# A message-passing block in fp32 on one core: another opening, plain points in the third group, the second period unrolled

## The reference

```
# layer 0, per graph, x: 256 x 128, A: 256 x 256
h      = relu(bn1(conv1d(x^T, conv1_w)))                # 1 tap
x_conv = relu(bn2(conv1d(h, conv2_w, pad=8)) + x^T)^T   # 17 taps, 128 -> 128 channels
s      = x @ w_se.T + b_se                              # 3 columns
A      = exp(-|s_n - s_m|^2) * adj
x_nmp  = A @ relu(x @ w_msg.T + b_msg)
gi     = [x_conv, x_nmp] @ w_ih.T + b_ih ; gh = x @ w_hh.T + b_hh
r, z   = sigmoid(gi_r + gh_r), sigmoid(gi_z + gh_z)
n      = tanh(gi_n + r * gh_n)
x      = layernorm(x + (1 - z) * n + z * x)
# layer 1
h      = relu(((1 + eps) * x + adj @ x) @ W1 + b1)
x      = layernorm(x + h @ W2 + b2)
```

## Time and profile before

| | |
|---|---|
| median of 3 runs | 387.81 us (386.9 to 388.11) |
| profiled execution | 386.43 us, its span 384.5 us |
| PE busy | 363.2 us (94%), 2150 matmuls |
| DVE busy | 326.4 us (85%), 669 instructions |
| ACT busy | 232.1 us (60%) |
| POOL busy | 222.5 us (58%) |
| DMA | 19.39 MB, mean 50 GB/s |

### The profile page before, as it was taken

How to read it: one execution, slowest core, us unless ns; L and a number is a source line. 1 busy time by engine, 2 the same in 40 slices (tenths; PEclk the granted TensorE clock), 3 DMA queues, 4 the chain that set the end, 5 groups by cost and what they waited for, 6 DMA issues and landing times.

```text
span 384.5 us, 6418 instructions
## 1 busy us (share of the span) xinstructions
PE 363.2 (94%) x2150; PEld 315.1 (82%) x2150; DVE 326.4 (85%) x669; ACT 232.1 (60%) x435; POOL 222.5 (58%) x195
## 2 busy tenths in 40 slices
PE   3969997999999999999999999999999999999994
PEld 1847876798888998989888898989888998988973
DVE  4999999999699986999689986999879996994584
ACT  4454445664866566673776558574676648555765
POOL 3246273698328763597437963396536983286352
PEclk9996999999999999999999999999999999999999
DMA  7500004030110210120101301130101201000002
GB/s 245 213 0 3 0 0 141 26 112 1 56 55 18 94 40 17 55 111 0 55 5 49 109 0 55 55 108 3 55 1 56 109 3 55 3 0 2 0 29 82
DMA packets 7991, 19.39 MB, mean 50 GB/s; under 512 B 672, under 2 KB 5024, under 8 KB 6944
## 3 DMA queue, kind: packets, MB, share of 16 engines
q1 hardware_dynamic: 7536, 18.50, 13.6%
q10 hardware_dynamic: 432, 0.59, 0.5%
HBM read 14.90 MB, written 4.19 MB: 50 GB/s over the span
## 4 chain that ended last, share of the span: by engine, by line
PE 61%; DVE 30%; issue 5%; DMA 1%; ACT 1%; POOL 1%; SPq 0%; DVEq 0%; ACTq 0%
PE back L1266 26%; PE conv L1266 17%; PE back L1379 6%; DVE stats L1015 3%; PE back L1474 3%; DVE stl L844 3%; DVE tail L1050 2%; PE front L1351 2%; DVE wl L1077 2%; DVE adjT L1120 2%; PE back L1430 2%; DVE sv L865 1%; DVE nmpl L844 1%; DMA tail<-in_conv_dram 1%; PE front L1371 1%
## 5 line engine op out<-in xcount | busy, mean ns | idle before, releaser
L1266 PE MATMUL conv<-sth,wh 128*128 128x256 f32 x217 | 65.4, 301 | 1.9 <-DVE stl L844 1.8
L1266 PE MATMUL conv<-stl,wh 128*128 128x256 f32 x217 | 61.8, 285 | 0.0
L1266 PE MATMUL conv<-sth,wl 128*128 128x256 f32 x217 | 61.7, 284 | 0.0
L538 POOL TENSOR_TENSOR rstd<-rstd,minus_half 128x4 f32<-128x4 f32 (+1 forms) x34 | 38.3, 1127 | 35.3 <-DVE rstd L1019 34.7
L559 POOL TENSOR_TENSOR amat<-amat,adjT 128x512 f32<-128x512 f32 x32 | 50.6, 1609 | 5.4 <-ACT amat L682 5.4
L543 POOL TENSOR_TENSOR xw<-xw,xv 128x512 f32<-128x512 f32 (+1 forms) x17 | 21.4, 1256 | 48.4 <-ACT xw L706 48.4
L1266 PEld LDWEIGHTS conv<-sth,wh 128*128 128x128 f32 x217 | 40.9, 189 | 4.6 <-DVE stl L844 1.7
L1266 PEld LDWEIGHTS conv<-stl,wh 128*128 128x128 f32 x217 | 41.1, 189 | 0.1
L1266 PEld LDWEIGHTS conv<-sth,wl 128*128 128x128 f32 x217 | 40.8, 188 | 0.0
L638 ACT ACTIVATE sth<-sv 128x272 fp32r<-128x272 f32 (+1 forms) x33 | 17.3, 523 | 33.6 <-DVE sv L865 21.5
L567 POOL TENSOR_TENSOR adjT<-adjT,diag 128x256 f32<-128x256 f32 x32 | 28.0, 903 | 8.0 <-DVE diag L1166 8.0
(11 more groups left out here) (232 smaller groups left out, 1033.0 us busy)
## 6 DMA issues: line engine op xcount, KB each, us to landing
adjT<-in_adj_dram SPq DMA_DIRECT2D x8, 1024.0 KB, 4.8
out_dram<-tail SPq DMA_DIRECT2D x15, 256.0 KB, 2.1
xv<-in_x_dram SPq DMA_DIRECT2D x7, 512.0 KB, 3.3
gbuf<-in_gates_dram SPq DMA_DIRECT2D x1, 576.0 KB, 7.4
tail<-in_conv_dram ACTq DMA_DIRECT2D x2, 256.0 KB, 4.0
xv<-in_x_dram SPq DMA_DIRECT2D x2, 256.0 KB, 4.8
later_w<-in_later_dram SPq DMA_DIRECT2D x1, 452.0 KB, 6.2
tail<-in_conv_dram SPq DMA_DIRECT2D x1, 320.0 KB, 5.2
```

What stands on the lines that cost most here:

```text
L538: done(pool.tensor_tensor(rstd[:, k, v, q], rstd[:, k, v, q], minus_half[:, q], ALU.pow), RSTD[k])
L1266: ins = pe.matmul(bank, a, b, start=first and k == 0, stop=last and k == len(todo) - 1)
```

## The change

Ten things, all in the opening and the first two periods:

1. Loads: the conv weights' first piece is issued before the second half of x; the third piece goes to ACT's queue; `later_w` is cut in two, the message part (264 columns) on ACT's queue, the second layer's part (semaphore `mlp_loaded`) on SP's behind x of group 1, where the identity also goes. SP no longer waits for the conv weights before it loads group 1's x.
2. `first_diffs(g)` makes both token differences on DVE, for groups 0 and 1; POOL makes none in the opening.
3. Group 0's PLUS1 and MINUS1 streams are made on DVE (`first_stream1`), between the tap sums.
4. On DVE `factors(0)` stands ahead of `parts1(0)`, the second x low part of group 0 behind `u_sum(0)`.
5. On PE the transposes of the factors stand ahead of MINUS2, and the four distances stand together behind it; ACT's exps follow them, with the tap copies behind.
6. `diag` is made by ACT from the identity; eps1 = 1 + eps in place in the vectors.
7. The combined taps of HALF and PLUS2 lie in `first_w` (which grows by nine blocks; PLUS2's lie over conv1's weights) and not in the gates' buffer. Their high parts are the last of ACT's opening, their low parts are made at the end of the second period's `pair1_add` (`second`), and group 2's HALF and PLUS2 points are plain.
8. In the first period `stream_low(1, 2)`, before in the opening, follows `parts1`; DVE's `gates` is cut into `reset` and `add_input`, with the low parts of taps between; `u_sum(1)` moves behind `h_low(0)`, `pair2_add(1)` behind the x splits.
9. On POOL the diagonal adds of group 0 wait in two pairs (for ACT's first `nmp_high` and for DVE's first message sum of group 1), and `x_low1` of group 1 moves into the first period, one half behind each of the two `rsqrt`.
10. The loop covers periods 3, 4 and 5, 6; the second period, steady(2), stands ahead of it.

The core of the diff:

```diff
             steady(1, 1, True)
+            steady(2, 0, True)
             with eng.Fori(0, (GROUPS - 4) // 2) as i:
-                steady(i * 2 + 2, 0, True)
                 steady(i * 2 + 3, 1, True)
-            steady(GROUPS - 2, 0, True)
+                steady(i * 2 + 4, 0, True)
...
-        W_ORDER = ("conv1", "gates", HALF, PLUS2, PLUS1, ZERO, MINUS2, MINUS1, INF, "w1")
+        W_ORDER = ("conv1", "gates", PLUS1, MINUS2, ZERO, MINUS1, INF, "w1", HALF, PLUS2)
...
 # SP prologue
                 sp.dma_start(xv[0][:, cols(0)], x_v[0, :, cols(0)]).then_inc(x_pair0_loaded, 16)
+                sp.dma_start(c2raw[:, 0:5, :], t["conv2"][:, 0:5, :]).then_inc(conv2_loaded, 16)
                 done(sp.dma_start(xv[0][:, cols(1)], x_v[0, :, cols(1)]), X_LOADED)
-                sp.dma_start(c2raw[:, 0:5, :], t["conv2"][:, 0:5, :]).then_inc(conv2_loaded, 16)
-                sp.dma_start(c2raw[:, 5:9, :], t["conv2"][:, 5:9, :]).then_inc(conv2_loaded, 16)
-                sp.dma_start(later_w[:, :], t["later"]).then_inc(later_loaded, 16)
-                sp.wait_ge(conv2_loaded, 64)
                 wait(sp, X_LOADED, 0, 16)
                 load_x(1, 1)
+                sp.dma_start(ident, t["consts"]).then_inc(consts_loaded, 16)
+                sp.dma_start(later_w[:, W1_AT:], t["later"][:, W1_AT:]).then_inc(mlp_loaded, 16)
...
 # DVE, steady
+                reset(gb, 0)
+                if first:
                     tap_low(MINUS2)
-                gates(gb, 1 - u, 0)
-                if first:
-                    tap_low(MINUS1)
+                add_input(gb, 0)
                 gates_end(gb, 0)
...
+                if second:
+                    tap_low(HALF)
+                    tap_low(PLUS2)
...
 # PE, steady
-                if not first:
+                if second:
+                    plain_taps(gm, HALF)
+                    taps(gm, ZERO)
+                    plain_taps(gm, PLUS2)
+                elif not first:
```

223 lines of the change are left out of this document (131 added, 92 removed).

## The result

The changed kernel takes 383.39 us, the median of four runs (383.15 to 383.65); the kernel before took 387.36 us in four runs (386.59 to 388.11). The ratio is 0.9898, 95% interval 0.9874 to 0.9921, so the gain is 4.0 us with an interval from 3.1 to 4.9. The forecast was 383.0, a gain of 4.8 against the median of 387.81 shown ahead. Timed again later the changed kernel took 383.24 us against 386.77 (ratio 0.9916, 0.99 to 0.9931), a gain of 3.5 us. Over the experiments 33 further runs of the kernel before have medians of 386.58 to 386.77, so the 387.36 above lies high, and the gain is nearer to 3.5 us than to 4.0.

A forecast was written before the change was run, and what follows sets the result against it. VectorE's instruction list was taken to bound until 93.67 us, TensorE afterwards. Opening -4.1, first period -1.5, plain points +0.3, second period +0.7, boundary wait -0.2 gave -4.8: 383.0 us from 387.81, range 379.9 to 386.2.

The forecast's parts named there:

- Loads: Opening: the new load order costs nothing, -0.3 to +0.5 us; x's second half is hidden if landed by about 7.7.
- DVE's first differences: Opening: DVE making both of group 0's token differences alone takes 1.3 us where one half took 1.89; -0.6 us.
- Taken off and put on DVE's list: Opening: weight splits, diag and a stream split leave DVE, -2.5 us; group 1's differences, two streams, x's low part come, +2.8.
- Masks: Opening: POOL's masks start near 25.6 us instead of 28.39 and hit DVE less; -0.7 us, from -1.6 to +0.5.
- Contention that goes: Opening: with POOL idle from 16 to 25 us, factor steps save 1.9 us and two tap sums 1.2; -3.1 us.
- First period with the plain points: First period -1.5 us from factor steps without POOL neighbours and earlier gates; group 2's unsplit HALF and PLUS2 points +0.3.
- Second period: HALF and PLUS2 low splits, now ahead of the first output sum, cost +0.7 us, from 0 to +2.6.
- Unrolling: Period loop: changing which bodies stand inside it costs 0 us, as the number of bodies in the code stays the same.
- Collisions come back: Rival, opening and first period: POOL's masks, streams and adds meet DVE's moved two-input instructions; 385.7 us, chance 0.20.
- DVE stops binding: Rival, opening and first period: POOL's work misses DVE almost wholly, only PE's work is left; 380.5 us, chance 0.13.
- Paid back: Rival: second period's splits cost 2.6 us and late PE gates lose half the opening's gain; 387.0 us, chance 0.07.
- The clock's case: Rival, opening before group 1's gates: PE pauses, its clock falls to half rate; slower, 389.5 us, chance 0.05.

The follow-up runs named there:

- experiment 10: Changed kernel with x's second half loaded before conv weights, both periods' low splits moved earlier, POOL's masks held until the last tap sum: 381.37 us, ratio 0.9869.
- Experiment 1: Changed kernel with the second half of group 0's x issued ahead of the first conv weights again: 383.53 us, ratio 0.992.
- Experiment 7: Changed kernel plus two POOL tensor operations on unread scratch beside DVE's group 0 factor steps: 385.74 us, ratio 0.9971.
- experiment 8: Changed kernel with half of group 0's and both of group 1's token differences back on POOL: 385.08 us, ratio 0.9962.
- Experiments 3: Changed kernel with POOL's two splits of group 1's x back behind the opening's diagonal adds: 383.81 us, ratio 0.9931.
- 6: Changed kernel with the low halves of INF's and W1's weights split earlier in the first period, before group 0's residual addition: 382.39 us, ratio 0.9889.
- Experiment 2: Changed kernel with the second period's HALF and PLUS2 low splits between reset product and first gates' add: 382.59 us, ratio 0.9893.
- experiment 11: Changed kernel with HALF and PLUS2 weights split in the opening, group 2's points split again, and the period loop as before: 383.61 us, ratio 0.9923.

## Why the prediction was right, and where its terms were off

The forecast of 383.0 us and its direction held, and so did the main mechanism: GpSimd's work beside VectorE's factor steps and tap sums went, and both early stretches became shorter. The gain is 4.0 us against 4.8; the terms were off by more than that, on both sides.

Part of the agreement is luck. Between the two profiled executions, for which the sum was made, the forecast was -4.8 and the result is -2.9, and 0.7 of that is a shortening of the later periods that the sum had at nothing. The medians show 4.0 because the kernel before ran high in those four runs; against its later medians the gain is 3.2 to 3.5 us.

**Loads: nothing forecast, +0.7 measured.** The bound I gave was +0.5, and "h1 later than 10.9 us" was named as a sign of error; DVE's first difference, for which it waits, starts at 11.53. The step that failed is "hidden if it lands by about 7.7 us": x's second half landed at 8.3. It cost PE more than the wait, too. PE's HALF point of group 0 starts 2.0 us later than before (15.78 for 13.78): conv1 ends 0.9 later (10.43 for 9.57), and the products between it and the point take 1.1 more. Here are the message products of the kernel before, of the changed kernel and of experiment 10 (count, busy us, mean ns):

```profile
L1351 PE MATMUL front<-later_w,xv 128*128 128x132 f32 x12 | 2.4, 372 | 0.0
```

```profile
L1400 PE MATMUL front<-later_w,xv 128*128 128x132 f32 x12 | 2.8, 427 | 0.0
```

```profile
L1407 PE MATMUL front<-later_w,xv 128*128 128x132 f32 x12 | 1.5, 276 | 0.0
```

The delay is still there when the PLUS2 point of group 0 starts (21.43 us for 19.56), which the distances and exps follow, and so the masks start at 27.5 and not at the 25.6 us that I gave. Experiment 1 gave that earlier start, and showed that it is worth 0.2 us at the end of the opening.

By the Trainium skill (DMA: Bandwidth & Descriptors, Issuing engines are not separate DMA queues) loads of several engines share the same 16 DMA engines and interleave. The trace fits that, with a landing anywhere from just ahead of 8.03 to 9.30 us in nine executions of one order; that the interleaving makes the landing loose is not shown by any run.

**DVE's first differences, -0.6: right.** Two in 1.36 us (11.53 to 12.89) where I gave 1.3.

**Taken off and put on DVE's list, -2.5 and +2.8: about right, but collisions were left out.** DVE's busy time in the opening fell by 4.1 us (39.34 to 35.26; its stretch begins in both at the first tap work, 8.33 and 8.36). Group 1's differences took 0.92 and 1.78 us beside the masks, 2.6 in place of 1.3, and x's second low part 1.24 in place of 0.7. These are hits by the masks, which the sum has in the next term.

**Masks, -0.7 forecast, -0.2 measured.** The term was mis-sized, and it doesn't follow from its own parts: one hit less is -0.9, the diagonal adds +0.6, together -0.3. In the trace three old hits went (the last tap sum 1.77 to 0.82, the first wv 1.50 to 0.43, the usum sum ahead of it 1.76 to 1.25, together -2.5), and new ones came: x's low part and the differences as above (+1.9), the last usum pair beside POOL's streams and diagonal adds 2.30 for 1.87 (+0.4).

**Contention that goes, -3.1: right.** Factor steps 2.91 to 0.97 (-1.9), two tap sums 2.85 to 1.67 (-1.2). Experiment 7 brings the neighbours back and the time with them. By experiment 8 the reason isn't the move of group 1's differences to DVE: in the new order its h1 is there only at 28.4 us, when the factor steps are long done, and the PLUS1 and MINUS1 streams need parts1, which now stands behind the factors. The order alone keeps both away from the factor steps.

**The sum of the opening, -4.1 forecast, -2.8 measured:** +0.7 from the loads, +0.5 from the masks term. TensorE's gates at 45.35 us stayed under the 45.5 that I gave as the limit.

**First period with the plain points, -1.2 forecast, -0.8 measured; the parts were wrong more than the sum.** The factor steps gave -2.6 (3.86 to 1.28) for -2.9, and the 2.0 us gate wait went. The collision that I feared for the pair sums, +1.3, didn't come: the masks of this period end at 76.73, and the pair takes 1.29 us at 79.42. Before, it took 3.46 us beside the masks and the x splits ahead of it 2.88, for 1.28 now, so here 3.8 us went that the forecast hadn't counted. The collision came 10 us earlier. POOL's x split, put between the norm steps, pushed POOL's additions and masks into DVE's low splits, and the three rows at 68.55 to 71.60 us cost some 3 us over what they take alone (4.70 in all). The INF stream's first step at 58.91 us meets POOL's gate product too, 1.51 us for 0.43. In all DVE's busy time fell by 2.0 us (43.88 to 41.90), and only 0.8 of that came: PE's waits fell from 3.7 to 2.9 us, and they set the period, not the sum of DVE's list, by which I had reckoned. I priced the moved split at its old place only; its new one I called free, "the x split between the norm steps". Experiments 3 and 6 show both ends: back at its old place it costs 0.4 more, and with the low weights out of its way 0.9 less.

By the Trainium skill (GPSIMD Engine Reference, Specifications) it is DVE instructions with two SBUF inputs, or in a two-port mode, that contend with POOL. The trace agrees: those three have two SBUF inputs, and the four usum rows at 73.62 us beside the masks, which read one input from PSUM, take 1.64 us together. Two inputs are not the only case: the cast in experiments 3 and 7 has one, and is stretched from 0.21 to 1.00 and 0.82 us; whether it runs in a two-port mode no run here shows. The rule was in my hands, and I applied it to the differences but not to the splits at 68 us.

**Second period, +0.7 forecast, +1.4 measured.** The mechanism is as written, with the size off (+1.0 forecast where the plain PLUS2 is counted here): the two splits take 2.69 us where I put 1.5 with a possible 0.6 on the second. They meet both of POOL's differences (1.65 and 1.91 us) and not only the first. PE's wait at group 3's PLUS2 (135.62 us) is 0.6 us, longer than 0.5 as forecast, and a wait of 0.8 stands ahead of its HALF at 131.44. Experiment 2 puts them elsewhere and gets 0.8 back.

**Unrolling, 0: the loop's place gave 0.2** (experiment 11). The later periods' -0.7 us I had named as a sign of error ("periods from the third on differ from 44.2 us"). They are 44.0, and for 0.5 us of it I have no cause.

**Rivals.** "Collisions come back" (385.7) is right in kind: three splits in the first period and two in the second met POOL. Its price was too high: it gave the first period no gain, where 0.8 us came, and 1.2 us of loss to the masks, where 0.5 came. "DVE stops binding" (380.5) is out: DVE still had 35.26 of 37.25 us. "Paid back" (387.0) is out: 1.4 us came back in the second period, and PE reached the gates in time. The clock's case didn't arise: the granted clock is 1.00 from 30 to 35 us, where it was 0.51. PE's pauses ahead of it were 1.00, 0.75 and 1.75 us before, and are one of 0.68 us now; in experiment 8 a pause of 2.07 us is followed by 0.50 again, and no other kernel with the new opening shows a fall there.

```profile
30.00:35.00 5.00, 4.93 (x23) 3.97 (x22) 4.93 (x7) 3.04 (x7) 3.41 (x3) 1.00 0.02 3
```
